# Sixteen-head attention: maxima of two heads as one pair of row tiles, and fixed groups of PSUM banks in place of a ring of three

## The chip, the core and the metric

The kernel runs on one core of a Trainium2 chip. The metric is the device time of one execution of the whole program, in microseconds (us), lower is better. The engines are TensorE (PE; its weight loads are shown apart as PEld), VectorE (DVE), ScalarE (ACT), GpSimd (POOL) and SyncE (SP). PSUM has eight banks of 512 float32 per partition; here they are `PS[:, 0]` to `PS[:, 7]`.

## The reference

Four layers of attention, cross attention and experts on `x` of 2 x 1024 x 256. The change concerns the six sublayers that run the class `Attention`: their tags are a0, a8, a9 and a11 (queries and keys are both the 1024 rows) and a4 and a10 (1024 queries, 154 keys of a context). a0 and a9 are causal; a10 has a mask. All have 16 heads of 16 elements. Cut to what they compute:

```python
q, k, v = ...                       # (b, s, 256) @ weights, split into 16 heads of 16
scores = einsum('bqhd,bkhd->bhqk', q, k) * scale    # scale is 1/4
probs = softmax(scores [+ causal or given mask])
out = einsum('bhqk,bkhd->bqhd', probs, v)
```

## The kernel before

**Precision.** A matmul of bfloat16 operands streams one column a cycle. So q and k are each cut into three bfloat16 parts (high, middle, low), and the six products of parts that matter are laid along the contraction: head h has its q in 96 rows of `qS[:, h, :]` and its k in 96 rows of `kS[:, h, :]`. Two more rows (`QH` to `QM`, 96 and 97) hold minus the row maximum in two parts in `qS`, and ones in `kS`, so that a score comes out with its maximum already taken away.

**Tiling.** A sublayer has four segments s (two batches, two halves of eight heads). A segment has four units u, (g, qb): four heads by 512 queries. A unit has steps t, one for each 128 keys: 8 without a causal mask, 4 or 8 with one, 2 where there are 154 keys. So a8 and a11 have 16 units and 128 steps, a0 and a9 have 96 steps, a4 and a10 have 32. Each step has two slots jj (two heads each).

**Pieces.** The work around the steps is cut into pieces:

- `split`: q, k, v of 128 rows for eight heads (`qkv`), read from PSUM by ACT (by DVE where there is a bias or a norm of q and k) into `A`, then cut into parts in `ST`: the high parts by ACT in segment 0 and by POOL from segment 1 on, the rest on DVE and POOL;
- `turn`: eight transposes of `ST` on PE into one bank, copied to `qS` or `kS` by ACT and DVE in turn;
- `max`: a score matmul with the queries on partitions (128 x 512 for one head), whose maximum over keys DVE takes with `tensor_reduce`;
- `fin1`, `fin2`: the maxima are cut into two parts, transposed and written to `qS`;
- `out`: the finished unit is transposed and divided by its sums.

**Order.** `place` deals the pieces to slots by position (`spread`); the maxima of unit u+1 go to slots of unit u. Every engine runs the same list. PE's slot is: two score matmuls (`pe_scores`), in the second slot of a step also the value matmuls of the step before (`pe_values`: float32, four column tiles of 32 side by side), then the slot's pieces. ACT takes the exponential of the two banks of a slot in one instruction. `self.first` comes ahead of all steps: the whole preparation of segment 0, then the maxima of unit 0, then `fin1`, `fin2`.

**Banks.** Scores use banks 0, 1 (slot 0) and 2, 3 (slot 1), values bank 4. All pieces share a ring of three, banks 5 to 7: `bank` gives `5 + use % 3`, and `wait_bank` makes PE wait until the piece three uses back has been read. A `max` piece fills one bank (or, with 154 keys, one bank with two heads side by side).

Of the kernel before, what the change touches and what calls it, by code (L numbers as in the profile page):

```python
# [15 lines left out]
S = 1024  # L16
# [428 lines left out]
class Attention(Stage):  # L445
# [12 lines left out]

    has_post = False
    lead = 0.3  # L460

    def __init__(self, K, tag, KV, causal):
# [10 lines left out]
        self.ST = [scr.take([2, 8, 104], BF16) for _ in range(3)]  # L473
# [14 lines left out]
    def place(self):  # L488
# [28 lines left out]
        order = list(self.first)  # L517
        for pieces in self.slots:
            order += pieces
        order.append(("out", len(self.units) - 1))  # L520
        self.use, self.by_use, self.turns = {}, [], {}
        for p in order:
            if p[0] != "fin1":
                self.use[p] = len(self.by_use)
                self.by_use.append(p)
            if p[0] == "turn":
                self.turns[p] = len(self.turns)
# [13 lines left out]
    def max_pieces(self, u):  # L541
        return [("max", u, i, half) for i in range(16 if self.KV == S else 8) for half in range(self.halves(u))]
# [9 lines left out]
    def bank(self, p):  # L552
        return 5 + self.use[p] % 3
# [4 lines left out]
    def wait_read(self, e, p):  # L558

        K, tag = self.K, self.tag  # L560
        on_act = (p[0] == "split" and self.bias is None and not self.has_post) or (p[0] == "turn" and self.turn_on_act(p))
        e.wait_ge(K.av if on_act else K.vv, (tag, "aux", p))
# [28 lines left out]
    def slot(self, ST, rows, z, js):  # L591
        v = ST[0:rows, z, :, 0:96].rearrange("p h (j d) -> p h j d", d=16)
# [4 lines left out]
    def dup(self, v, rows, n):  # L597
        return bc(v[0:rows].unsqueeze(2), [rows, 8, n, 16])
# [22 lines left out]
    def pe_piece(self, e, p):  # L621
# [7 lines left out]
        elif p[0] == "turn":  # L629
# [7 lines left out]
            for h in range(8):  # L637
                t = e.transpose(pb[0:104, h, 0:rows], ST[0:rows, z, h, :], K.identb[0:rows, 0:rows])
            t.then_inc(K.mm, (tag, p))
        elif p[0] == "max":  # L640
            _, u, i, half = p
            s, g, qb = self.units[u]
            b, qS, kS = s // 2, self.qS[s % 2], self.kS[s % 2]
            o = self.max_bank(p)
            self.wait_turned(e, s)
            if self.KV == S:
                qt, j = i // 4, i % 4
                h, q0 = 4 * g + j, 512 * qb + 128 * qt
                diag = self.causal and half == self.halves(u) - 1
                m = e.matmul(o, qS[0:QH, h, q0:q0 + 128], kS[0:QH, h, 512 * half:512 * half + o.shape[1]], start=True, stop=not diag)  # L650
                if diag:
                    m = e.matmul(o[:, o.shape[1] - 128:o.shape[1]], K.identb, K.maskS, start=False, stop=True)
            else:
                qt, jj = i // 2, i % 2
                q0 = 512 * qb + 128 * qt
                for k in range(2):
                    h = 4 * g + 2 * jj + k
                    m = e.matmul(o[:, KC * k:KC * k + KC], qS[0:QH, h, q0:q0 + 128], kS[0:QH, h, 0:KC], start=True, stop=self.mask is None)
                    if self.mask is not None:
                        m = e.matmul(o[:, KC * k:KC * k + KC], K.identb, self.mask[0][:, 8 * b + 4 * qb + qt, :], start=False, stop=True)  # L660
# [13 lines left out]
    def max_bank(self, p):  # L674

        _, u, i, half = p
        width = 2 * KC
        if self.KV == S:
            diag = self.causal and half == self.halves(u) - 1
            width = 128 * (i // 4 + 1) if diag else 512  # L680
        return self.K.PS[:, self.bank(p), 0:width]
# [6 lines left out]
    def pe_scores(self, e, n, jj):  # L688
        K, tag, PS = self.K, self.tag, self.K.PS
# [6 lines left out]
        if n > 0:  # L696
            e.wait_ge(K.av, (tag, "exp", n - 1, jj))
        if t == 0:
            self.wait_read(e, ("fin2", u))
        for k in range(2):  # L700
            h = 4 * g + 2 * jj + k
            o = PS[0:rows, 2 * jj + k, lo:512]
            m = e.matmul(o, self.kS[s % 2][0:QM, h, 128 * t:128 * t + rows], self.qS[s % 2][0:QM, h, q0 + lo:q0 + 512], start=True,
                         stop=not diag and self.mask is None)
            if self.mask is not None:
                m = e.matmul(o, K.identb[0:rows, 0:rows], self.mask[1][0:rows, t, b * S + q0:b * S + q0 + 512], start=False, stop=True)
            if diag:
                m = e.matmul(PS[0:rows, 2 * jj + k, lo:lo + 128], K.identb, K.maskT, start=False, stop=True)
# [32 lines left out]
    def act_piece(self, e, p):  # L741
        K, tag, PS = self.K, self.tag, self.K.PS
        if p[0] == "split":
# [26 lines left out]
            if hq:  # L770
                m = e.activation(self.slot(ST, rows, 0, [0, 1, 2]), self.dup(a[:, 0], rows, 3), ACT.Copy)
                m.then_inc(K.av, (tag, "hi" if not hk else "hi q", s, w))
# [3099 lines left out]
```

## Time and profile before

| | us |
|---|---|
| median of three runs | 7174.8 (7172.98 to 7180.21) |
| the profiled execution | 7183.6, of it 7181.8 in the span of the trace |

The profile's page gives the busy time of each engine, as a share of the span:

| engine | busy us | share |
|---|---|---|
| PE | 5763.3 | 80% |
| PEld (weight loads) | 3029.1 | 42% |
| DVE | 4253.9 | 59% |
| ACT | 2749.3 | 38% |
| POOL | 1762.4 | 25% |

PE leads, but the mean covers unlike stages. The six sublayers stand in the trace as follows (read from the order of time on PE): for each the preparation of segment 0, the maxima of unit 0, and the steps.

| tag | keys | preparation from | maxima from | steps from, to | length of the steps |
|---|---|---|---|---|---|
| a0 | 1024, causal | 39 | 70 | 80, 437 | 357 |
| a4 | 154 | 2205 | 2220 | 2227, 2397 | 171 |
| a8 | 1024 | 4512 | 4536 | 4559, 5027 | 468 |
| a9 | 1024, causal | 5490 | 5522 | 5532, 5899 | 366 |
| a10 | 154, mask | 5950 | 5975 | 5982, 6189 | 206 |
| a11 | 1024 | 6247 | 6279 | 6302, 6773 | 472 |

Together that is about 2040 us of steps and 220 us ahead of them. The other 4900 us run code that the change doesn't touch. PE's clock is shown as a granted share: 1.00 is 2.4 GHz, 0.50 is 1.2 GHz.

### The profile page before, as it was taken

To read this page: it belongs to the slowest core of one execution; us is meant where nothing else is said; L and a number is where in the kernel's file an instruction comes from. 1 tells how busy PE (TensorE), PEld (TensorE's weight loads), DVE (VectorE), ACT (ScalarE), POOL (GpSimd) and SP (SyncE) were. 2 spreads that over 40 slices of the span, in tenths; PEclk is the share of its full clock that TensorE was granted. 3 is DMA by queue.
4 is the path that set the end of the run, shared out by engine and by line. 5 is a ranking of instruction groups with operands and counts; after the bars stand their busy time and mean duration, and the time that the engine had idled before them with its cause. 6 is when DMAs were issued, how large, how long until landed. Compare 5 with 4: busy or idle time off the path is not lost. (4 is left out here: it accounts for less than half of the span.)

```text
span 7181.8 us, 69269 instructions
## 1 busy us (share of the span) xinstructions
PE 5763.3 (80%) x26178; PEld 3029.1 (42%) x26194; DVE 4253.9 (59%) x7193; ACT 2749.3 (38%) x4376; POOL 1762.4 (25%) x2107
## 2 busy tenths in 40 slices
PE   7969999999877865656566687899694887799966
PEld 4435555555534432323222255332582444433344
DVE  5664454444365469898998922777225765587622
ACT  4543333333204333333333321567112555456500
POOL 2211121211013015353444500220204213222022
PEclk9989999999888987888787886899797998899988
DMA  1000000000000000000000000000351000000022
GB/s 45 1 2 1 1 1 1 1 1 1 18 9 17 7 24 0 0 0 0 0 0 0 0 9 15 22 1 1 109 182 33 1 15 1 27 1 1 26 92 86
DMA packets 47884, 134.60 MB, mean 19 GB/s; under 512 B 4822, under 2 KB 31990, under 8 KB 41534
## 3 DMA queue, kind: packets, MB, share of 16 engines
q1 hardware_dynamic: 38094, 77.67, 3.1%
q0 software_dynamic: 9456, 52.50, 2.1%
q8 instruction: 207, 3.39, 0.2%
q14 instruction: 127, 1.04, 0.0%
HBM read 99.42 MB, written 31.20 MB: 18 GB/s over the span
## 5 line engine op out<-in xcount | busy, mean ns | idle before, releaser
L73 PE MATMUL PS<-SC 128*32 128x512 f32 (+12 forms) x11760 | 2703.7, 464 | 625.9 <-DVE SC L82 500.6
L79 ACT ACTIVATE SC<-PS 128x512 f32<-128x512 f32 (+10 forms) x2773 | 1900.8, 716 | 1967.2 <-PE PS L73 1622.1
L94 DVE TENSOR_REDUCE SC<-PS 128x1 f32<-128x512 f32 (+4 forms) x2832 | 1567.5, 594 | 697.4 <-PE PS L73 682.6
L73 PEld LDWEIGHTS PS<-SC 128*32 128x32 f32 (+5 forms) x11760 | 988.7, 122 | 1933.9 <-DVE SC L82 617.1
L73 PE MATMUL PS<-AR 128*128 128x512 f32 (+6 forms) x3902 | 1219.0, 424 | 106.9 <-DVE SC L82 55.2
L82 POOL TENSOR_TENSOR SC<-SC 128x128 bf16<-128x128 f32 (+4 forms) x764 | 935.2, 1232 | 1070.5 <-ACT SC L79 749.3
L76 PE MATMUL PS<-AR,SC 128*104 128x128 bf16 (+4 forms) x4820 | 579.4, 265 | 499.9 <-DVE SC L85 228.4
L73 PE MATMUL PS<-SC,AR 128*128 128x512 f32 (+7 forms) x1824 | 861.1, 602 | 61.9 <-DVE SC L82 20.6
L91 DVE TENSOR_TENSOR_SCAN SC<-SC 128x512 f32<-128x512 f32 (+1 forms) x544 | 885.7, 1689 | 14.9 <-ACT SC L79 3.5
L73 PEld LDWEIGHTS PS<-AR 128*128 128x128 f32 (+2 forms) x3902 | 631.7, 178 | 529.9 <-issue 334.3
L79 ACT ACTIVATE SC<-SC 128x512 f32<-128x512 f32 (+5 forms) x874 | 440.5, 561 | 1015.4 <-DVE SC L91 741.7
L76 PEld LDWEIGHTS PS<-AR,SC 128*104 128x104 bf16 (+4 forms) x4820 | 444.5, 140 | 747.7 <-issue 398.2
L73 PE MATMUL PS<-RR 97*128 97x512 f32 (+4 forms) x2048 | 630.6, 440 | 3.4 <-DVE SC L94 2.9
L73 PEld LDWEIGHTS PS<-SC,AR 128*128 128x128 f32 (+3 forms) x1840 | 387.1, 218 | 474.7 <-issue 361.2
L97 POOL CAST SC<-SC 128x256 bf16<-128x256 f32 (+2 forms) x696 | 263.1, 405 | 1212.4 <-DVE SC L82 622.0
L82 DVE TENSOR_TENSOR SC<-PS,SC 128x256 f32<-128x256 f32 (+4 forms) x529 | 239.3, 463 | 432.4 <-PE PS L73 229.1
L73 PEld LDWEIGHTS PS<-RR 97*128 97x128 f32 (+3 forms) x2048 | 372.4, 186 | 213.9 <-issue 123.0
L73 PE MATMUL PS<-AR,SC 128*128 128x256 f32 (+3 forms) x1504 | 417.6, 430 | 28.8 <-ACT SC L79 16.2
L97 POOL CAST RR<-SC 64x512 fp32r<-64x512 f32 (+1 forms) x305 | 168.5, 553 | 997.3 <-DVE SC L82 972.6
L97 DVE COPY SC<-PS 2x512 bf16<-2x512 bf16 (+7 forms) x405 | 216.4, 534 | 275.5 <-PE PS L73 139.4
L73 PEld LDWEIGHTS PS<-AR,SC 128*128 128x128 f32 (+1 forms) x1504 | 283.5, 196 | 140.0 <-issue 89.2
L82 DVE TENSOR_TENSOR SC<-SC,PS 128x2048 f32<-128x2048 f32 (+2 forms) x176 | 304.9, 1732 | 28.1 <-PE PS L73 27.0
(71 smaller groups left out, 2049.5 us busy)
## 6 DMA issues: line engine op xcount, KB each, us to landing
xg<-AR SPq DMA_DIRECT2D x20, 512.0 KB, 5.4
SC<-in_pk11e SPq DMA_DIRECT2D x8, 1152.0 KB, 6.5
SC<-in_pk11e SPq DMA_DIRECT2D x8, 1028.0 KB, 5.1
SC<-xg SPq DMA_DIRECT2D x23, 256.0 KB, 2.9
yg<-SC SPq DMA_DIRECT2D x23, 256.0 KB, 2.2
SC<-xg SPq DMA_DIRECT2D x8, 512.0 KB, 6.1
yg<-SC SPq DMA_DIRECT2D x8, 512.0 KB, 3.3
AR<-in_pk SPq DMA_DIRECT2D x2, 1562.0 KB, 8.5
```

What stands on the lines that cost most here:

```text
L73: return Step(self.real and self.real.matmul(*a, **k))
L76: return Step(self.real and self.real.transpose(*a, **k))
L79: return Step(self.real and self.real.activation(*a, **k))
L82: return Step(self.real and self.real.tensor_tensor(*a, **k))
L91: return Step(self.real and self.real.tensor_tensor_scan(*a, **k))
L94: return Step(self.real and self.real.tensor_reduce(*a, **k))
L97: return Step(self.real and self.real.tensor_copy(*a, **k))
```

## The change

**Layout.** `ST` grows from 104 to 112 columns. An even head keeps its parts in rows 0 to 95 and its maximum in 96 and 97; an odd head has its maximum in rows 0 and 1 and its parts in 16 to 111, in reversed order. With that, three of the six products (48 rows) of an even head lie in rows 0 to 47 and those of an odd head in rows 64 to 111.

**Maxima.** A `max` piece now takes two heads: one matmul on rows 0 to 47, one on rows 64 to 111. In the built program they are row tiles of 64 x 128, at positions (0, 0) and (64, 0), and write two banks. One `tensor_reduce` takes both maxima (two outputs per partition). The maximum is then that of three products of six; the same value is taken from every score of the row, so the softmax stays the same. There are 1152 such pieces in all six sublayers.

**Banks.** `queue` deals three rings: scores (banks 0, 1 and 2, 3 in turn, as before), maxima (the one pair 5, 6), and the rest, `split`, `turn`, `fin2`, `out` (the one bank 7). `wait_bank` looks two uses back for scores and one use back for the other two.

**Parts.** All instructions that cut into parts are issued for even heads and for odd heads apart: with half the elements, and twice as many.

```diff
 def bank(self, p):
-        return 5 + self.use[p] % 3
+        z, n = self.ring[p]
+        return (2 * (n % 2), 5, 7)[z]
...
 def wait_bank(self, e, p):
-        n = self.use[p] - 3
+        z, n = self.ring[p]
+        n -= (2, 1, 1)[z]
         if n >= 0:
-            self.wait_read(e, self.by_use[n])
+            self.wait_read(e, self.rings[z][n])
...
+            for k, r in ((0, slice(0, 48)), (1, slice(64, 112))):
+                h = 4 * g + 2 * jj + k
+                m = e.matmul(o[:, k, :], qS[r, h, q0:q0 + 128], kS[r, h, k0:k0 + w], start=True, stop=not diag and self.mask is None)
+            for k in range(2):
+                if self.mask is not None:
+                    m = e.matmul(o[:, k, :], K.identb, self.mask[0][:, 8 * b + 4 * qb + qt, :], start=False, stop=True)
                 if diag:
-                    m = e.matmul(o[:, o.shape[1] - 128:o.shape[1]], K.identb, K.maskS, start=False, stop=True)
+                    m = e.matmul(o[:, k, w - 128:w], K.identb, K.maskS, start=False, stop=True)
...
 def max_bank(self, p):
+        return self.K.PS[:, self.bank(p):self.bank(p) + 2, 0:width]
...
 def act_piece(self, e, p):
-            if hq:
-                m = e.activation(self.slot(ST, rows, 0, [0, 1, 2]), self.dup(a[:, 0], rows, 3), ACT.Copy)
...
-            if hk:
-                e.activation(self.slot(ST, rows, 1, [0, 3]), self.dup(a[:, 1], rows, 2), ACT.Copy).then_inc(K.av, (tag, "hi k", s, w))
-                e.activation(self.slot(ST, rows, 1, [5]), a[0:rows, 1], ACT.Copy).then_inc(K.av, (tag, "hi", s, w))
+            for odd in range(2):
+                if hq:
+                    e.activation(self.slot(ST, rows, 0, odd, [1, 2, 3]), self.some(a, rows, 0, odd, 3), ACT.Copy).then_inc(
...
+                if hk:
+                    e.activation(self.slot(ST, rows, 1, odd, [0, 2, 4]), self.some(a, rows, 1, odd, 3), ACT.Copy).then_inc(
...
 def dve_piece(self, e, p):
-                e.tensor_reduce(m2[:, i // 4, i % 4, half:half + 1], o, AX.X, ALU.max).then_inc(K.vv, (tag, "aux", p))
...
+            e.tensor_reduce(self.m2[u % 2][:, qt, 2 * jj:2 * jj + 2, half], self.max_bank(p), AX.X, ALU.max).then_inc(K.vv, (tag, "aux", p))
```

Apart from this, the scratch of the first norm and one row of biases get other places in memory.

**PE, steps of a8 between two preparations.** `128x512` with a wait for DVE is a `max` matmul, `128x512` with a wait for ACT opens the two score matmuls of a slot, `32x512 x4` are the value matmuls. Before:

```order
L73 MATMUL PS<-SC 128x512 [waits s_dve_results] x2
L73 MATMUL PS<-SC 128x512 [waits s_act_results]
L73 MATMUL PS<-SC 128x512
L73 MATMUL PS<-SC 32x512 x4
L73 MATMUL PS<-SC 128x512 [waits s_dve_results] x2
L73 MATMUL PS<-SC 128x512 [waits s_act_results]
L73 MATMUL PS<-SC 128x512
```

With the change:

```order
L73 MATMUL PS<-SC 128x512 [waits s_act_results]
L73 MATMUL PS<-SC 128x512
L73 MATMUL PS<-SC 32x512 x4
L73 MATMUL PS<-SC 128x512 [waits s_dve_results]
L73 MATMUL PS<-SC 128x512
L73 MATMUL PS<-SC 128x512 [waits s_act_results]
L73 MATMUL PS<-SC 128x512
L73 MATMUL PS<-SC 128x512 [waits s_dve_results]
L73 MATMUL PS<-SC 128x512
```

Where two maxima stood, each with a wait on the read three uses back, there is one pair of row tiles with one wait, on the read of the pair just before it.

**PE, preparation of segment 0 in a8.** `128x384` is the `split`, `104x128` (`112x128`) the eight transposes of a `turn`. Before:

```order
L73 MATMUL PS<-AR 128x384 [waits s_act_results]
L73 MATMUL PS<-AR 128x384
L76 MATMUL PS<-AR,SC 104x128 [waits s_pool_results,s_act_results]
L76 MATMUL PS<-AR,SC 104x128 x7
L76 MATMUL PS<-AR,SC 104x128 [waits s_dve_results]
L76 MATMUL PS<-AR,SC 104x128 x7
```

With the change:

```order
L73 MATMUL PS<-AR 128x384 [waits s_dve_results]
L73 MATMUL PS<-AR 128x384
L76 MATMUL PS<-AR,SC 112x128 [waits s_pool_results,s_act_results]
L76 MATMUL PS<-AR,SC 112x128 x7
L76 MATMUL PS<-AR,SC 112x128 [waits s_act_results]
L76 MATMUL PS<-AR,SC 112x128 x7
```

The order is the same, but every wait now names the reader of the piece just before: a split waits for DVE's copy of the turn ahead of it, the second turn for ACT's copy of the first.

**ACT, preparation of segment 0 in a0.** `128x8x16` and `128x256` read a split from PSUM, the next rows write its high parts, `98x8x128` (`112x8x128`) copies a turn. Before:

```order
L79 ACTIVATE SC<-PS 128x8x16
L79 ACTIVATE SC<-PS 128x256
L79 ACTIVATE SC<-SC 128x8x48
L79 ACTIVATE SC<-SC 128x8x2x16
L79 ACTIVATE SC<-SC 128x8x16
L79 ACTIVATE SC<-PS 98x8x128
```

With the change:

```order
L79 ACTIVATE SC<-PS 128x8x16
L79 ACTIVATE SC<-PS 128x256
L79 ACTIVATE SC<-SC 128x4x48
L79 ACTIVATE SC<-SC 128x4x3x16
L79 ACTIVATE SC<-SC 128x4x48
L79 ACTIVATE SC<-SC 128x4x3x16
L79 ACTIVATE SC<-PS 112x8x128
```

Between the read of a split and the copy of a turn stand four instructions in place of three, each with 192 elements per partition.

## Rows read from the trace of the kernel before

**Rows 1.** Stretches: length, busy us of each engine (count), granted clock, DMA, GB/s
```profile
4700.00:4800.00 100.00, 96.64 (x593) 34.20 (x591) 76.94 (x134) 67.78 (x81) 20.55 (x51) 1.00 0.00 1
```

**Rows 2.** Groups of DVE by shape, whole span: count, busy us, mean ns, idle before
```profile
L94 DVE TENSOR_REDUCE SC<-PS 128x1 f32<-128x512 f32 x1920 | 1246.9, 685 | 530.1 <-PE PS L73 522.9
L94 DVE TENSOR_REDUCE SC<-PS 128x2 f32<-128x308 f32 x256 | 112.6, 474 | 39.7 <-PE PS L73 36.8
L94 DVE TENSOR_REDUCE SC<-SC 128x64 f32<-128x1024 f32 x8 | 9.8, 1220 | 0.3
```

**Rows 3.** Order of time, PE, a8: start, us, instruction
```profile
4670.14 0.38 PE L73 MATMUL PS<-SC 98*128 98x512 bf16 x1
4670.45 0.64 PE L73 MATMUL PS<-SC 128*32 128x512 f32 x4
...
4671.45 0.39 PE L73 MATMUL PS<-SC 96*128 96x512 bf16 x1
```

**Rows 4.** Order of time, first maxima of a8, PE and DVE
```profile
4536.14 0.38 PE L73 MATMUL PS<-SC 96*128 96x512 bf16 x1 [0.88 <-DVE SC L97]
...
4536.55 0.69 DVE L94 TENSOR_REDUCE SC<-PS 128x1 f32<-128x512 f32 x1 [0.56 <-PE PS L73]
...
4537.30 0.10 PEld L73 LDWEIGHTS PS<-SC 96*128 96x128 bf16 x1 [0.85 <-DVE SC L94]
```

**Rows 5.** Order of time, PE where tile sizes change, a10 and a0
```profile
6183.30 0.39 PE L73 MATMUL PS<-SC 98*26 98x512 bf16 x1
6183.61 0.38 PE L73 MATMUL PS<-SC,AR 26*26 26x512 bf16 x1
...
275.61 0.70 PE L73 MATMUL PS<-AR,SC 64*128 64x256 f32 x2
276.24 0.34 PE L73 MATMUL PS<-SC 98*128 98x384 bf16 x1
```

**Rows 6.** Order of time, PE: `out` pieces of a8, then a4; unit ends of a0
```profile
4727.01 0.55 PE L76 MATMUL PS<-AR,SC 128*128 128x128 f32 x3 [0.21 <-DVE SC L94]
...
4849.10 0.55 PE L76 MATMUL PS<-AR,SC 128*128 128x128 f32 x3 [0.21 <-DVE SC L94]
...
4936.02 0.55 PE L76 MATMUL PS<-AR,SC 128*128 128x128 f32 x3 [0.21 <-DVE SC L94]
...
4961.70 0.55 PE L76 MATMUL PS<-AR,SC 128*128 128x128 f32 x3 [0.21 <-DVE SC L94]
...
2361.70 0.52 PE L76 MATMUL PS<-AR,SC 128*128 128x128 f32 x3 [0.39 <-ACT SC L79]
2369.64 0.52 PE L76 MATMUL PS<-AR,SC 128*128 128x128 f32 x3 [0.39 <-ACT SC L79]
...
270.85 0.69 PE L73 MATMUL PS<-SC 128*32 128x128 f32 x9
366.47 0.69 PE L73 MATMUL PS<-SC 128*32 128x128 f32 x9
```

**Rows 7.** Order of time, preparation of a8, PE, then ACT
```profile
4523.81 1.51 PE L73 MATMUL PS<-AR 128*128 128x384 f32 x4
4525.28 1.10 PE L76 MATMUL PS<-AR,SC 128*104 128x128 bf16 x16
4526.22 1.51 PE L73 MATMUL PS<-AR 128*128 128x384 f32 x4
...
4520.88 0.52 ACT L79 ACTIVATE SC<-SC 128x384 bf16<-128x384 f32 x1
...
4521.62 0.29 ACT L79 ACTIVATE SC<-SC 128x128 bf16<-128x128 f32 x1
4521.82 1.00 ACT L79 ACTIVATE SC<-PS 98x1024 bf16<-98x1024 bf16 x1
```

**Rows 8.** Stretches of 8 us in a4 and in the first maxima of a8
```profile
2352.00:2360.00 8.00, 6.23 (x53) 2.88 (x56) 5.99 (x18) 5.79 (x8) 0.00 (x0) 1.00 0.00 0
4544.00:4552.00 8.00, 8.00 (x14) 1.36 (x13) 8.00 (x14) 0.00 (x0) 0.00 (x0) 0.50 0.00 0
```

More of the change, by code:

```diff
@@ L516, in place, with queue, read_by_act @@
         self.first = self.prep(0) + self.max_pieces(0) + [("fin1", 0), ("fin2", 0)]
[L517 to L527, printed above, removed]
+        self.ring, self.rings, self.turns = {}, ([], [], []), {}
+        for p in self.first:
+            self.queue(p)
+        for n in range(len(self.steps)):
+            for jj in range(2):
+                self.queue(("score", n, jj))
+                for p in self.slots[2 * n + jj]:
+                    self.queue(p)
+        self.queue(("out", len(self.units) - 1))
+    def queue(self, p):
+        if p[0] == "turn":
+            self.turns[p] = len(self.turns)
+        if p[0] != "fin1":
+            z = {"score": 0, "max": 1}.get(p[0], 2)
+            self.ring[p] = (z, len(self.rings[z]))
+            self.rings[z].append(p)
+    def read_by_act(self, p):
+        return (p[0] == "split" and self.bias is None and not self.has_post) or (p[0] == "turn" and self.turn_on_act(p))
     def spread(self, pieces, a, b, rank=0):
@@ L560, in wait_read @@
         K, tag = self.K, self.tag
-        on_act = (p[0] == "split" and self.bias is None and not self.has_post) or (p[0] == "turn" and self.turn_on_act(p))
-        e.wait_ge(K.av if on_act else K.vv, (tag, "aux", p))
+        if p[0] == "score":
+            e.wait_ge(K.av, (tag, "exp", p[1], p[2]))
+            return
+        e.wait_ge(K.av if self.read_by_act(p) else K.vv, (tag, "aux", p))
         if p[0] == "fin2":
@@ L644, in pe_piece @@
             o = self.max_bank(p)
+            w = o.shape[2]
+            q0, k0 = 512 * qb + 128 * qt, 512 * half
+            diag = self.causal and half == self.halves(u) - 1
             self.wait_turned(e, s)
[L646 to L650, printed above, removed]
[L651 to L660 removed]
+            for k, r in ((0, slice(0, 48)), (1, slice(64, 112))):
[4 more added lines that the diff above has]
+                    m = e.matmul(o[:, k, :], K.identb, self.mask[0][:, 8 * b + 4 * qb + qt, :], start=False, stop=True)
+                if diag:
+                    m = e.matmul(o[:, k, w - 128:w], K.identb, K.maskS, start=False, stop=True)
             m.then_inc(K.mm, (tag, p))
@@ new lines, in pool_piece @@
+        e.wait_ge(K.gv, (tag, "mid k" if hk else "mid q", 1, s, w))
+        for odd in range(2):
+            if hq:
+                m = e.tensor_tensor(self.slot(ST, rows, 0, odd, [4]), self.some(a, rows, 0, odd, 1), self.slot(ST, rows, 0, odd, [0]), ALU.subtract)
+                m.then_inc(K.gv, (tag, "parts" if odd and not hk else ("lo q", odd), s, w))
+            if hk:
+                m = e.tensor_tensor(self.slot(ST, rows, 1, odd, [3]), self.some(a, rows, 1, odd, 1), self.slot(ST, rows, 1, odd, [1]), ALU.subtract)
+                m.then_inc(K.gv, (tag, "parts" if odd else "lo k", s, w))
```

116 lines of the change are left out of this document (57 added, 59 removed).

## The prediction, made before the changed kernel was timed

> **What bounds the kernel now.** I first cut the span into stretches of 100 us. In the steps of a8, PE is busy for 96.6 of 100 us at the full clock, and DVE for 76.9 [rows 1]; a11 reads alike. So PE sets the pace of the two sublayers without a causal mask, with DVE not far behind. Next the order of time within a step. A 512-column matmul streams 0.21 us at 2.4 GHz; the value matmuls of a step take 1.00 us from their start to the next piece's, and they start 0.31 us after a score matmul that streams 0.21 [rows 3]. Four scores, four maxima, values: 1.7 + 0.1 + 1.0, about 2.9 us, and a unit of eight steps without preparation takes 25.7 us from one `out` to the next; four units, three of them with preparation, take 122.1 [rows 6]. Then the groups of DVE by shape: a reduce of 512 takes 0.685 us, of 308 0.474, and one of 1024 columns 1.22 (from SBUF, but 0.685 plus 512 times the slope between the first two, 1.03 ns, gives 1.22 as well) [rows 2].
>
> What lets PE stay busy is the ring of three banks: PE makes two more maxima while DVE reads one. In the first maxima of a8, where nothing else runs, a reduce starts 0.41 us after its matmul does, and PE's next weight load comes 0.06 us after the reduce that freed the bank (4536.55 + 0.69 to 4537.30) [rows 4].
>
> **The change, part by part.**
>
> *Pairs.* PE drops 1152 maxima matmuls' worth of streaming if the two row tiles run side by side: 640 of 512 columns (0.213 us each), 256 causal ones of 320 on average, 256 of 154. That is 136 + 34 + 16 = 186 us of PE work. That row tiles overlap is not in the trace; the nearest are the column tiles of the values: four float32 matmuls within 0.64 us [rows 3], where one alone would stream 0.43 or more. I take them as side by side and bound it by one after the other.
>
> *Tile sizes.* A pair is 64 x 128 between 128-row matmuls. In a10, matmuls that alternate between tile sizes start 0.31 us apart in place of 0.21: 0.10 us for each change of size. In a0 two float32 matmuls on 64 rows take 0.63 us, no more than four 128-column ones beside them, so the price may be zero [rows 5]. I take 0.10. A step of a8 has two changes now (around the values) and five then: 0.3 us more against 0.43 saved. So PE's own gain is a third of what it looks like, 0 to 0.43 us a step.
>
> The Trainium skill, TensorEngine Tiling (Array Packing), Tiling Modes, says that a change of tiling mode, unlike a change of tile, drains TensorE. The rows of a10 agree (0.10 us), those of a0 leave it open. By the rule nearly nothing of PE's gain is left; without it 0.3 us a step would be, but in a chain that DVE paces that moves the sum little.
>
> *One pair of banks for maxima.* This is the term that decides. PE can't start a pair before DVE has read the last. From pair to pair: 0.44 us to the reduce's start (0.41 and a little for the second tile), 1.22 for 1024 columns, 0.09 back to PE: **1.75 us**, whatever PE does meanwhile. PE behind that wait holds up scores, values, exponentials. Sixteen pairs are 28.0 us a unit, more than the 25.7 a unit takes now. And the pairs aren't evenly loaded: where only two scores stand between them, PE needs 0.22 + 0.10 + 0.43 + 0.10 = 0.85 and waits 0.9; with the values 1.84, all PE. A unit without preparation, pair by pair from the order of the pieces: nine gaps of 1.75, four of 1.84, one with `fin2` 2.1, one with `out` 2.45, and one that spans three slots without maxima 3.8: **31.5 us for 25.7**. With preparation I add 1.3 for each split and 0.47 for each turn [rows 7] where they don't fit under 1.75, and 0.4 where DVE's copy of a turn goes ahead of a reduce: four units 139 for 122. Three such groups, +52; three and a half units without, +16; the start +3: 71 us for a8, 142 with a11. Bounds: 80 (only 28.0 a unit, the preparation hidden) to 190.
>
> *Causal, a0 and a9.* The diagonal pairs add two mask matmuls and two changes of size; with 128, 256, 384, 512 columns a pair takes 0.99, 1.31, 1.63, 1.95 us, so 16 pairs of a unit of eight tiles 25.8 us, 8 of a short unit 11.8. The chain is densest in each group of four units, where 32 pairs fall in 20 slots: in a0's last group 37 us pass for them now (377 to 414 in the trace, DVE busy for nearly all of it), then 2 x 25.8 and DVE's other work, 56, and 2.5 more ahead: +21.5. In the three groups with preparation, each 95.6 us [rows 6], PE's work already fills that stretch; +12 each (2 to 20). So +57 for a0, 115 with a9. Bounds 60 to 150.
>
> *154 keys, a4 and a10.* A pair is as wide as before, but the three-deep ring is gone: 0.29 + 0.474 + 0.09 = 0.85 us from pair to pair. A unit without preparation takes 7.9 us [rows 6]; then six gaps of 0.85, 2.5 with `fin2`, 2.8 with `out`: 10.3. Twenty splits and turns of a segment fall in two units, one after another in the one bank 7, each waiting some 0.6 us for ACT or DVE to read the last. +45 a sublayer, 90 for both. Bounds 35 to 130.
>
> *One bank for the rest, ahead of the steps.* Before the first step nothing hides bank 7. Now a tile of a8 takes 2.4 us (4523.81 to 4526.22) [rows 7]. Then: split 1.5, ACT's read 0.7, ACT's four high parts 1.3 (192 columns each, between 0.29 for 128 and 0.52 for 384) while PE turns, ACT's copy 1.0, second turn 0.7, DVE's copy 0.7, handovers 0.2: 6.1 us. Eight tiles, the first and last shorter: +23; the maxima of unit 0 at 1.75 for 1.2 per pair: +9. With the same count: a0 +24, a4 +16, a8 +32, a9 +33, a10 +16, a11 +34: **155**. Bounds 90 to 190.
>
> *Parts on POOL.* Twice the instructions, each for half the elements, about 1 us more per split. POOL is busy for 20.6 of 100 us in the steps [rows 1] and a split comes every 10 us or so: nothing. If that cover went, `turn` would wait for POOL.
>
> *Clock.* In the first maxima of a8, where DVE paces PE, the clock was at 0.50 (1.2 GHz); in a4, whose waits are short, at 1.00 [rows 8]. The longer start of six sublayers looks like the former: half of 155 + 36 us at the low level, where PE's part doubles, +40 (0 to 70). Whether the steps follow is a rival.
>
> **Sum.** 142 + 115 + 90 + 155 + 40 = 542 us. The profiled execution took 7183.6, so 7725; the median of the runs is 8.8 lower: **7717 us**, +7.6%.
>
> **Rivals.**
>
> - *Waits partly hidden.* Every term at its low bound: 80 + 60 + 35 + 90 + 0 = 265, so 7440. For it: sums of gaps assume that PE catches up nothing. Against: 16 times 1.75 is above a unit's time today. Chance 0.17.
> - *The clock falls in the steps too.* At 1.2 GHz a gap with values is 3.5 us and the other 1.95: 14 us more a unit. If half of the 30 units of a8 and a11 run so, and as much of a0 and a9, +310: 8030. For it: PE will stand still for half of every other gap, as in the maxima at 0.50. Against: a4's stretch at 1.00 has waits as well. Chance 0.15.
> - *The two tiles run one after the other.* Each pair 0.21 us longer in the chain, on 0.8 of them: +150, 7870. Chance 0.10.
> - *Faster.* PE's work decides alone, all 186 us are saved, and no wait for DVE shows. It needs the reduce (1.22) plus handovers to fit into PE's other work in each gap, and changes of size to be free: 6989. Decided by whether PE's work between pairs is over 1.75 us; it is so only in gaps with values. Chance 0.03.
>
> The Trainium skill, TensorE: Matmul & The Clock Gate, Packing small matmuls, reports 3.07 times for four row tiles of 512 columns, not 4. By that a pair would stream some 0.28 us (an estimate), and 1152 pairs would add at most 80 us to the chain.
>
> **Numbers.** The forecast holds 0.55. The range leaves out what lies under 7470 and over 8040, about one case in ten on either side. Under 0.2% (14 us, about what a measurement of this kernel can tell) is neither: faster 0.03, same 0.01, slower 0.96.
>
> **What the changed profile would show.** In a8: PE busy near 70% and not 97; reduces `128x2<-128x1024` near 1.22 us, 1.7 apart, each starting 0.44 us after its pair; PE idle "<- DVE L94" about 0.9 us once a step; 31 us from `out` to `out`. In the preparation: splits 6 us apart. Two row tiles starting together, or 0.21 us apart, settle that rival; the granted clock of 100 us stretches settles the other. The forecast is wrong if PE's waits for L94 sum up to little, or if a reduce of two banks takes well under 1.2 us.

## The result, and the profile after

The changed kernel takes 7994.2 us (median of four runs, 7988.05 to 8001.16) where the kernel before took 7173.9 in the same comparison: 1.114 times as long, with a 95% interval of 1.112 to 1.116. That is 820 us more; the prediction had 542 more. The profiled execution's span is 7986.1 us, against 7181.8 before.

First the whole: busy time of each engine, with the share of the span, from the page of the changed kernel.

```profile
PE 6022.7 (75%) x26178; PEld 3048.7 (38%) x26194; DVE 4236.8 (53%) x6349; ACT 2770.4 (35%) x4424; POOL 1903.6 (24%) x3097
```

The pairs were to save PE work, and PE is busy for 259 us more. So something made its work slower, beside the waits. The stretches say where: 100 us of a8, of a4 and of a0 (length, busy us with count of PE, PEld, DVE, ACT, POOL, then the granted clock).

```profile
5100.00:5200.00 100.00, 80.00 (x453) 22.83 (x454) 61.94 (x68) 54.80 (x62) 16.04 (x55) 0.91 0.00 1
2400.00:2500.00 100.00, 72.86 (x405) 35.92 (x400) 35.46 (x92) 35.93 (x43) 34.19 (x121) 0.67 0.00 1
300.00:400.00 100.00, 85.96 (x640) 39.10 (x638) 49.83 (x73) 52.56 (x78) 27.67 (x95) 0.82 0.00 1
```

In a8 PE was busy for 96.6 us of 100 and DVE for 76.9 [rows 1]; now it is 80.0 and 61.9. No engine is full any more: they wait for each other. In a4 and a0 the clock has gone too.

Cut by sublayer, the two traces give this (us; "ahead" is preparation and maxima of unit 0, the two parts of the steps are what PE is idle and what it is busy):

| tag | ahead, more by | steps before | steps after | more by | of it PE idle | of it PE busy | clock in the steps, before and after |
|---|---|---|---|---|---|---|---|
| a0 | 32.2 | 356.9 | 462.1 | 105.2 | 48.8 | 56.4 | 0.98, 0.77 |
| a4 | 19.5 | 170.7 | 286.4 | 115.7 | 47.4 | 68.3 | 0.93, 0.67 |
| a8 | 42.6 | 468.3 | 567.0 | 98.7 | 99.2 | -0.5 | 0.99, 0.93 |
| a9 | 36.8 | 367.0 | 451.8 | 84.8 | 53.1 | 31.6 | 0.98, 0.84 |
| a10 | 20.9 | 206.4 | 320.9 | 114.5 | 50.4 | 64.2 | 0.99, 0.80 |
| a11 | 40.5 | 471.9 | 565.6 | 93.7 | 99.7 | -5.9 | 0.99, 0.93 |

Sums: 193 ahead, 613 in the steps, of which 399 idle and 214 busy. The rest of the program is unchanged to a few us. (Ahead of the steps the kernel before takes 239 us by the table of its sublayers, and not the 220 that the sentence under it has.)

Now the chain, in the steps of a8. PE's order of time (start, us, instruction), then DVE's reduces in the same stretch:

```profile
5321.06 0.39 PE L73 MATMUL PS<-SC 48*128 48x512 bf16 x2 [0.78 <-DVE SC L94]
5321.38 0.39 PE L73 MATMUL PS<-SC 98*128 98x512 bf16 x1
5321.61 0.38 PE L73 MATMUL PS<-SC 112*128 112x512 bf16 x1
5321.92 0.64 PE L73 MATMUL PS<-SC 128*32 128x512 f32 x4
...
5322.92 0.39 PE L73 MATMUL PS<-SC 48*128 48x512 bf16 x2
5323.24 0.39 PE L73 MATMUL PS<-SC 98*128 98x512 bf16 x1
5323.46 0.38 PE L73 MATMUL PS<-SC 112*128 112x512 bf16 x1
5324.63 0.39 PE L73 MATMUL PS<-SC 48*128 48x512 bf16 x2 [0.78 <-DVE SC L94]
...
5321.49 1.22 DVE L94 TENSOR_REDUCE SC<-PS 128x2 f32<-128x1024 f32 x1 [0.49 <-PE PS L73]
5323.35 1.22 DVE L94 TENSOR_REDUCE SC<-PS 128x2 f32<-128x1024 f32 x1 [0.64 <-PE PS L73]
```

A pair is one row with x2 and 0.39 us, the same 0.39 that one matmul has alone: both row tiles run side by side. The score behind it starts 0.32 us later, 0.22 of streaming and 0.10 for the change of tile size. The reduce starts 0.43 us after its pair and takes 1.22, and the next pair comes 0.06 us behind it: 1.71 us from pair to pair (5322.92 to 5324.63), and 1.86 with the values between (5321.06 to 5322.92). PE's waits in the steps of a8 (in total, times, longest), now and before:

```profile
PE PS L73 <- DVE SC L94: 102.9, 123, 1.4
```
```profile
PE PS L73 <- DVE SC L94: 4.6, 23, 0.2
```

The prediction's signs, one by one: the distance of 1.75 us is there, the wait for L94 is 0.80 us a step (0.9 expected), and an `out` of a unit without preparation comes 31.2 us after the last (5362.14 and 5393.30; 31.5 expected, 25.7 before [rows 6]). PE's busy share in a8 is 80%, where near 70 was expected, and ahead of its steps a tile takes 5.7 to 7.7 us from split to split, for 6. The two `out`:

```profile
5362.14 0.33 PE L76 MATMUL PS<-AR,SC 128*128 128x128 f32 x1
...
5393.30 0.33 PE L76 MATMUL PS<-AR,SC 128*128 128x128 f32 x1
```

The granted clock is what isn't as expected. This is one unit of a4 without preparation, after and then before: the stretch, and PE's waits in it.

```profile
2630.63:2644.26 13.63, 10.03 (x49) 3.08 (x48) 5.85 (x15) 5.85 (x7) 0.00 (x0) 0.63 0.00 1
PE PS L73 <- DVE SC L94: 3.6, 5, 1.3
```
```profile
2378.66:2386.51 7.85, 6.08 (x49) 2.74 (x49) 5.41 (x15) 5.98 (x8) 0.00 (x0) 1.00 0.00 0
PE PS L73 <- ACT SC L79: 1.1, 1, 1.1
PE PS L73 <- DVE SC L94: 0.3, 1, 0.3
```

PE has 49 matmuls in both. They take 6.08 us at a clock of 1.00 (2.4 GHz), and 10.03 at 0.63, which is mostly 1.2 GHz. Of the 5.8 us that the unit grows, 4.0 are PE's own work at the lower clock (by estimate 6.08 us at 0.63 would be 9.7), and the waits are only the rest.

### The profile page after: what moved, and what is told of

It reads as the page before. It is cut to its first block and busy times, and to the rows that moved or that the text cites. A ratio compares the mean times of both kernels' runs of the same rounds, so it can differ in the third digit from the quotient of the medians.

```text
span 7986.1 us, 69289 instructions
## 1 busy us (share of the span) xinstructions
PE 6022.7 (75%) x26178; PEld 3048.7 (38%) x26194; DVE 4236.8 (53%) x6349; ACT 2770.4 (35%) x4424; POOL 1903.6 (24%) x3097
## 5 line engine op out<-in xcount | busy, mean ns | idle before, releaser
L73 PE MATMUL PS<-SC 128*32 128x512 f32 (+13 forms) x11760 | 2728.4, 503 | 1009.5 <-DVE SC L82 498.0
L94 DVE TENSOR_REDUCE SC<-PS 128x2 f32<-128x1024 f32 (+6 forms) x1936 | 1533.2, 802 | 1227.5 <-PE PS L73 1221.7
L73 PEld LDWEIGHTS PS<-SC 128*32 128x32 f32 (+6 forms) x11760 | 905.3, 124 | 2435.8 <-DVE SC L94 786.7
L73 PE MATMUL PS<-AR 128*128 128x512 f32 (+6 forms) x3902 | 1260.2, 448 | 176.6 <-DVE SC L82 81.2
L82 POOL TENSOR_TENSOR SC<-SC 128x64 bf16<-128x64 f32 (+4 forms) x1256 | 1005.2, 822 | 1078.2 <-ACT SC L79 744.9
L76 PE MATMUL PS<-AR,SC 128*112 128x128 bf16 (+4 forms) x4820 | 659.0, 288 | 589.2 <-DVE SC L85 229.8
L76 PEld LDWEIGHTS PS<-AR,SC 128*112 128x112 bf16 (+4 forms) x4820 | 497.7, 160 | 889.6 <-issue 428.9
L79 ACT ACTIVATE SC<-SC 128x512 f32<-128x512 f32 (+6 forms) x918 | 444.4, 543 | 1043.3 <-DVE SC L91 741.9
L97 POOL CAST SC<-SC 128x128 bf16<-128x128 f32 (+2 forms) x1176 | 326.7, 318 | 1697.1 <-DVE SC L82 897.7
L82 DVE TENSOR_TENSOR SC<-PS,SC 128x256 f32<-128x256 f32 (+5 forms) x465 | 219.9, 478 | 446.2 <-PE PS L73 240.5
```

The source lines that it names most:

```text
L73: return Step(self.real and self.real.matmul(*a, **k))
L76: return Step(self.real and self.real.transpose(*a, **k))
L79: return Step(self.real and self.real.activation(*a, **k))
L82: return Step(self.real and self.real.tensor_tensor(*a, **k))
L94: return Step(self.real and self.real.tensor_reduce(*a, **k))
L97: return Step(self.real and self.real.tensor_copy(*a, **k))
```

## The experiments

The change has four parts: who shares which bank, two heads read by one reduce, row tiles in place of full rows, and the finer cutting into parts. The runs take them one at a time. Six of them and the changed kernel stand in this table (us; the kernel before was 7172 to 7178 beside them; the run with full rows and two heads has the layout and the parts of the kernel before):

| maxima matmul | piece | ring of three (banks 5 to 7) | maxima 5, 6 and the rest 7 |
|---|---|---|---|
| full rows | one head | 7264 | 7675 |
| full rows | two heads, one reduce | | 8058 |
| row tile | one head | 7515 | 7950 |
| row tiles | two heads | 7555 (two reduces) | 7994 (one reduce, the changed kernel) |

**Banks alone.** The kernel before, its layout and full rows, with the changed kernel's pieces of two heads and its groups of banks.

```diff
-        return 5 + self.use[p] % 3
+        z, n = self.ring[p]
+        return (2 * (n % 2), 5, 7)[z]
...
+            for k in range(2):
+                h = 4 * g + 2 * jj + k
+                m = e.matmul(o[:, k, :], qS[0:QH, h, q0:q0 + 128], kS[0:QH, h, k0:k0 + w], ...)
```

> The kernel before, with its layout, its six products on 96 rows, and its way of cutting into parts, but with the changed kernel's pieces of two heads, one reduce of two banks, and its groups of banks (maxima 5 and 6, the rest 7). The banks part of the change alone. Theory (banks are the cost): the two matmuls of a pair run one after the other, so pair to pair is 0.65 + 1.22 + 0.09 = 1.96 us in a8; steps of a8 550 to 600 (468 before, 567 changed); 7900 to 8150 us. Rival (row tiles or the parts are the cost): 7174 to 7500.

Measured: 8058.2 us, 1.122 (1.120 to 1.124). The banks part alone costs 886 us, more than the whole change. Steps of a8, then of a9 (stretch, then PE's waits):

```profile
4873.03:5473.97 600.94, 476.83 (x2616) 152.32 (x2617) 339.08 (x369) 320.31 (x375) 78.39 (x192) 0.93 0.00 1
PE PS L73 <- DVE SC L94: 108.6, 120, 1.3
...
6016.11:6483.90 467.79, 370.62 (x2568) 163.98 (x2569) 250.66 (x385) 208.16 (x287) 78.92 (x192) 0.84 0.00 1
PE PS L73 <- DVE SC L94: 64.9, 81, 1.8
```

a8 takes 601 us, just over the expected 550 to 600. There is no row tile here, and the clock of a9 is at 0.84 as in the changed kernel: waits by themselves are enough to lower it.

**The ring of three back, row tiles kept, one head a piece.**

```diff
-            z = {"score": 0, "max": 1}.get(p[0], 2)
+            z = {"score": 0}.get(p[0], 1)
...
-        return (2 * (n % 2), 5, 7)[z]
+        return (2 * (n % 2), 5 + n % 3)[z]
...
-        n -= (2, 1, 1)[z]
+        n -= (2, 3)[z]
...
+            r, h = (slice(0, 48), slice(64, 112))[j % 2], 4 * g + j
+            m = e.matmul(o, qS[r, h, q0:q0 + 128], kS[r, h, k0:k0 + w], ...)
```

> The changed kernel, but a maxima piece is one head (one row tile, one bank, one reduce of 512 or less), even and odd head next to each other, and all pieces share one ring of three banks again, as before the change. Only row tiles, three products and the finer cutting into parts stay. Theory (the fixed groups of banks cost the time: a pair waits 1.22 us of reduce with nothing else to write, and bank 7 alone holds up the preparation): PE's waits for DVE's reduces fall from 103 us to under 15 in the steps of a8, preparation takes what it took before, clock back near 0.98; 7150 to 7250 us. Rival (row tiles and their changes of tile size are the cost): waits fall, but PE's busy time goes up, 7400 or more. Second rival (row tiles save 186 us of PE work as soon as waits are gone): 7050 or less.

Measured: 7514.8 us, 1.048 (1.046 to 1.050). The waits went as the theory said (5.0 us for L94 in a8), and 480 us came back, but not the other 340. The first rival is nearer: row tiles have a price of their own. The next run isolates it.

**The same with full rows.** Only the rows of the maxima matmul differ from the run above.

```diff
-            r, h = (slice(0, 48), slice(64, 112))[j % 2], 4 * g + j
+            r, h = slice(0, 112), 4 * g + j
```

> As the run with one head a piece over the ring of three (7515 us), but the maxima matmuls take all 112 rows of a head in place of a row tile of 48: the rows of the maximum still hold zeros then. Same pieces, same banks, same waits, same layout and same cutting into parts; no row tiles and no change of tile size around the maxima. Theory (row tiles themselves cost in that run: they run one after another, each group of them between two changes of tile size, and the clock of a0, a4, a9 and a10 falls with them): steps of a8 back to 468 to 472, clock of a0 and a9 back to 0.98, 7180 to 7240 us. Rival (the cutting in two halves and the odd heads' layout cost it): 7400 or more.

Measured: 7263.8 us, 1.012 (1.010 to 1.013). 251 us are the row tiles'. Steps of a9, with row tiles and then with full rows:

```profile
5665.90:6110.42 444.52, 422.00 (x2568) 164.39 (x2569) 264.69 (x569) 208.22 (x287) 99.49 (x336) 0.81 0.00 1
PE PS L73 <- DVE SC L94: 9.0, 26, 0.9
```
```profile
5588.97:5957.04 368.07, 323.26 (x2568) 147.02 (x2569) 259.53 (x569) 205.74 (x287) 99.72 (x336) 0.99 0.00 1
PE PS L73 <- DVE SC L94: 15.9, 49, 0.9
```

Both have 2568 matmuls on PE. With row tiles PE waits less for the reduces (9.0 us for 15.9), and still the clock is 0.81 in place of 0.99 and the steps are 76 us longer. So more waits aren't needed for a low clock: row tiles between full-row matmuls bring it too. In a8 the clock stays at 0.99 with both, and the steps are 481.1 and 469.1. With full rows a0, a8, a9 and a11 take what they took before (359.0, 469.1, 368.1, 471.3), so the new layout and the finer parts cost next to nothing in the steps, as predicted; outside all steps the two traces differ by 13 us. The 86 us that this run is slower than before are mostly in a4 and a10, 41 and 27 us, where one head a piece makes two reduces of 154 columns (0.314 us each) out of one of 308 (0.477) and takes two places of the ring for one. That this is the reason wasn't tested.

**The groups of banks, one head a piece.** With row tiles, and with full rows:

```diff
-        return (2 * (n % 2), 5, 7)[z]
+        return (2 * (n % 2), 5 + n % 2, 7)[z]
...
-        n -= (2, 1, 1)[z]
+        n -= (2, 2, 1)[z]
```

> The changed kernel with its own groups of banks (scores 0 to 3, maxima 5 and 6, the rest 7), but a maxima piece is one head with one bank and a reduce of its own, so a bank comes free 0.69 us after its reduce starts and not 1.22. Theory (the chain of pair, reduce of two banks, pair is what holds PE up in the steps): two reduces take 1.37 us a pair and each bank has its own chain of 0.41 + 0.69 + 0.09 = 1.19, so the chain is shorter than PE's own work in a8: waits for reduces fall from 103 to under 30 us, steps of a8 from 567 to about 490, a11 the same; a0 and a9 some 50 less each, and the clock follows; preparation in segment 0 unchanged (bank 7 is): 7600 to 7750 us. Rival (the number of banks for maxima counts, two in place of three, not how they are released): steps of a8 above 540, 7900 us.

> As the run with full-row maxima, one head a piece (7264 us), but with the changed kernel's groups of banks: scores 0 to 3, maxima 5 and 6, the rest 7. Against the run of the same groups with row tiles (7950 us) only the row tiles differ, and against the banks alone with a reduce of two banks (8058 us) only that each bank is read and freed by itself. Theory (the fixed groups cost mostly by the wait for a reduce of two banks and by bank 7, and the row tiles by PE's time and clock): a8 490 to 500, a0 and a9 375 to 390, preparation as changed, 7550 to 7650 us. Rival (two banks for maxima in place of three cost as much however they are read): 7850 or more.

Measured: 7949.9 us, 1.108 (1.106 to 1.110), and 7675.3, 1.070 (1.068 to 1.071). Both are above what I expected. Full rows first: against 8058 for the banks alone, 383 us came back with each bank read and freed by itself (the layout and the parts differ too, which cost next to nothing in the steps of the run above); a8 takes 512.6 us (490 to 500 expected). Against 7264 with the ring of three, two banks for maxima and one for the rest still cost 411. With row tiles the theory failed: 44 us came back, not 250 to 400, and a8 takes 542.9 us, as the rival had it (above 540), though by another way than the rival's. PE's waits for L94 in a8 did fall, to 47 us, but its busy time rose from 451 to 486. Each tile now waits for its own bank, and only 89 times in a8 do two row tiles start together, against 240 in the changed kernel. Where they don't, it looks like this:

```profile
5345.06 0.39 PE L73 MATMUL PS<-SC 48*128 48x512 bf16 x1 [0.24 <-DVE SC L94]
5345.65 0.39 PE L73 MATMUL PS<-SC 48*128 48x512 bf16 x1 [0.21 <-DVE SC L94]
```

**Bank 7 ahead of the steps.** The changed kernel, with the preparation of segment 0 dealt over banks 5, 6, 7.

```diff
         z, n = self.ring[p]
+        if z == 2 and n < self.ahead:
+            return 5 + n % 3
...
-        n -= (2, 1, 1)[z]
+        n -= 3 if z == 2 and n < self.ahead else (2, 1, 1)[z]
```

> The changed kernel, but the preparation of segment 0, ahead of all steps, deals its splits and turns over the three banks 5, 6, 7, which nothing else uses then. Theory (ahead of the steps the one bank 7 is what costs): a tile of a8 falls from 7.7 us to about 2.5 to 3.5, the six preparations lose 100 to 146 us together, nothing else moves: 7850 to 7900 us. Rival (twice as many instructions for the parts on ACT, DVE and POOL are the cost, or the clock): a tile stays at 6 us or more, 7950 to 7994.

Measured: 7849.7 us, 1.094 (1.092 to 1.096), 144 less than the changed kernel: as expected, and so is the tile of a8. In the changed kernel one tile stretches from split to split, 7.66 us; here it is 2.62 (PE, start, us):

```profile
4796.55 2.93 PE L73 MATMUL PS<-AR 128*128 128x384 f32 x4 [0.78 <-DVE SC L97]
...
4800.12 1.10 PE L76 MATMUL PS<-AR,SC 128*112 128x128 bf16 x8 [0.64 <-ACT SC L79]
...
4802.33 1.10 PE L76 MATMUL PS<-AR,SC 128*112 128x128 bf16 x8 [1.11 <-ACT SC L79]
...
4804.21 1.01 PE L73 MATMUL PS<-AR 128*128 128x384 f32 x1 [0.79 <-DVE SC L97]
```
```profile
4747.89 1.51 PE L73 MATMUL PS<-AR 128*128 128x384 f32 x4
...
4749.57 1.10 PE L76 MATMUL PS<-AR,SC 128*112 128x128 bf16 x16 [0.17 <-ACT SC L79]
...
4750.51 1.51 PE L73 MATMUL PS<-AR 128*128 128x384 f32 x4
```

Three waits a tile (0.64, 1.11, 0.78) are gone, and the split takes 1.51 us and not 2.93: with the waits the clock came back as well.

**Pairs side by side over three banks.** Row tiles in pairs again, but a pair takes two places of the ring and has two reduces.

```diff
+            self.rings[z].extend([p + (0,), p + (1,)] if p[0] == "max" else [p])
...
-        return (2 * (n % 2), 5, 7)[z]
+        return (2 * (n % 2), 5 + (n + k) % 3)[z]
...
+        for m in (n, n + 1)[0:2 if p[0] == "max" else 1]:
```

> The changed kernel, with its pairs of row tiles, but all pieces share the ring of three banks again, a pair takes two places of it, and DVE reads each head with a reduce of its own, so that the next pair can start when the first of two banks is read. Against the run with one head a piece (7515 us, a8's steps 481) only this differs: the two matmuls of a pair stand next to each other without a wait between them. Theory (row tiles run side by side only when nothing stands between them, and then save 0.43 us a step against three more changes of tile size of 0.10): a8 and a11 take about 450 in place of 481, a0 and a9 some 10 to 15 less, 7420 us, and the rest of the distance to 7174 is the clock in the causal sublayers and those with 154 keys. Rival (the two tiles do not overlap at all): 7500 to 7530.

Measured: 7555.4 us, 1.054 (1.052 to 1.056): slower than one head a piece. Steps of a8, pairs and then single heads:

```profile
4712.67:5218.88 506.21, 436.93 (x2617) 131.74 (x2617) 351.96 (x609) 319.75 (x375) 99.01 (x336) 0.96 0.00 1
PE PS L73 <- DVE SC L94: 58.9, 112, 0.9
```
```profile
4674.96:5156.05 481.09, 466.03 (x2616) 136.55 (x2617) 347.04 (x609) 320.33 (x375) 98.70 (x336) 0.99 0.00 1
PE PS L73 <- DVE SC L94: 5.0, 24, 0.4
```

PE's work did shrink, by 29 us, as the tiles run side by side. It is given back in waits: a pair needs two of three banks at once. I had compared PE's work with its own work only, and forgotten that the third bank is what hid the reduce.

**Hybrid, and another order on PE.** The kernel before in a0, a4, a9 and a10; in a8 and a11 pairs over the ring of three. The second of these runs then also changes PE's order within a step:

```diff
             for jj in range(2):
                 self.pe_scores(e, n, jj)
-                if jj == 1 and n > 0:
-                    self.pe_values(e, n - 1)
-                for p in self.slots[2 * n + jj]:
-                    self.pe_piece(e, p)
+            for p in self.slots[2 * n]:
+                self.pe_piece(e, p)
+            if n > 0:
+                self.pe_values(e, n - 1)
+            for p in self.slots[2 * n + 1]:
+                self.pe_piece(e, p)
```

> The kernel before in a0, a4, a9 and a10, and in a8 and a11 the changed layout with pairs of row tiles, but over the ring of three banks with a reduce for each head. Theory: as the run with pairs over three banks in a8 and a11 (about 450 in place of 468 and 472) and as before elsewhere: 7130 to 7160 us, faster than both. Rival (the parts in two halves and the changes of tile size take the gain): 7175 to 7210.

> As the run that has the kernel before in a0, a4, a9, a10 and pairs over three banks in a8 and a11 (7267 us), but in a8 and a11 PE's step is both slots' scores, a pair, the values, a pair, in place of scores, pair, scores, values, pair. The distance from pair to pair is then 1.3 to 1.4 us both times and no longer 0.85 and 1.84. Theory (that run lost to uneven gaps: a pair needs two of three banks, and where only two scores stand between pairs PE waits 0.5 us for DVE): waits for reduces fall from 60 us to under 25, a step goes to 2.8 to 2.95 us, steps of a8 and a11 to 430 to 450: 7110 to 7140 us, faster than before. Rival (DVE, 1.37 us a pair and more with its other work, becomes the bound, or the clock falls): a8 470 or more, 7180 to 7270.

Measured: 7266.6 us, 1.013 (1.011 to 1.015), slower than theory and rival alike, and 7182.8, 1.0006 (0.9997 to 1.0015). The uneven gaps were most of the cause in the first: with even ones the waits halve (59.7 to 27.7 us in a8), and the steps go from 505.2 to 464.3, where the kernel before has 468.3. The theory's 430 to 450 isn't reached, though:

```profile
4933.00:4981.95 48.95, 44.39 (x272) 11.81 (x272) 45.24 (x79) 34.57 (x39) 0.00 (x0) 1.00 0.00 1
```

These are two units without preparation, 24.5 us each (25.7 before). DVE is busy for 45.2 us of 49 and PE for 44.4: as the rival had it, DVE's two reduces a pair are the next bound, close behind PE.

**First maxima over the score banks.** As the last run, and the 16 pairs ahead of the steps of a8 and a11 use banks 0 to 3, with one reduce each.

```diff
+            z = 2 if p[0] == "max" and p[1] == 0 else {"score": 0}.get(p[0], 1)
...
-        return (2 * (n % 2), 5 + (n + k) % 3)[z]
+        return (2 * (n % 2), 5 + (n + k) % 3, 2 * (n % 2) + k)[z]
```

> As the run with the other order in a8 and a11 (7183 us), but the maxima of unit 0 in these two, ahead of the steps, take the score banks 0, 1 and 2, 3 in turn, which are free until the first step, with one reduce of two banks for a pair. Theory (these 16 pairs are bound by DVE: 1.22 us in place of two times 0.69, and no wait for a third bank): the maxima take 20 to 21 us in place of 26.4, and 22.6 in the kernel before: 7170 us, 0.1% under the kernel before, together with the 4 and 6 us that the other order saved in the steps. Rival (the chain of PE and DVE is what counts there, and the clock at 1.2 GHz): 24 us or more, 7180.

Measured: 7175.3 us beside 7175.2 for the kernel before, ratio 0.9998 (0.9989 to 1.0007). The first maxima of a8 fell from 26.4 to 21.5 us, those of a11 from 27.0 to 21.6. Of these 10 us some 5 show in the total (the run above was 4.7 us over the kernel before beside it, this one is level with it); the gain over the kernel before can't be told from none. This is the best version found, and it does not beat the kernel before.

**Does more work keep the clock up?** The changed kernel, with every score matmul of a4 and a10 issued twice.

```diff
+            for again in range(2 if self.KV != S else 1):
+                m = e.matmul(bank[:, lo:512], ...)
```

> The changed kernel, but in a4 and a10 every score matmul is issued twice with the same operands (the second overwrites the first), four more matmuls a step of 512 columns: 27 us more PE work in each of the two at the full clock, 55 at half. Everything else is as changed. Theory (in a4 and a10 most of the loss is the clock, which falls because PE stands still between short pieces of work): more work keeps the clock up, PE busy no more than now, steps of a4 from 286 to 240-265 and of a10 from 321 to 280-300, 7900 to 7950 us: more work, less time. Rival (the waits alone cost the time, and the clock falls for another reason): a4 and a10 get 27 to 55 us longer each, 8050 to 8100.

Measured: 8041.6 us, 1.122 (1.120 to 1.123), 47 more than the changed kernel. Steps of a4, twice and then once:

```profile
2381.41:2686.02 304.61, 228.83 (x1233) 97.89 (x1233) 105.93 (x276) 108.59 (x126) 68.55 (x240) 0.73 0.00 1
PE PS L73 <- DVE SC L94: 39.5, 56, 1.4
```
```profile
2383.61:2670.05 286.44, 208.71 (x1104) 91.78 (x1105) 106.05 (x276) 108.05 (x126) 68.68 (x240) 0.67 0.00 1
PE PS L73 <- DVE SC L94: 39.4, 56, 1.4
```

My theory falls. The clock rose a little, 0.67 to 0.73 and in a10 0.80 to 0.83, and the added work, 27 us in each at the full clock, cost 18 and 30 us: some 9 were won back in a4 and none in a10, far from a gain. The waits for L94 are the same to 0.1 us: filling in matmuls ahead of a wait does not remove the wait.

## Why the prediction was right in kind and short in size

The measured 7994 us lie in the stated range of 7470 to 8040, near its upper end and 277 over the forecast of 7717. The parts, one by one:

**One pair of banks (142 forecast, 192 measured).** The chain was right in each part: 0.43 + 1.22 + 0.06 for 0.44 + 1.22 + 0.09, a unit without preparation at 31.2 for 31.5. So were the last four units, three and a half with maxima: they grew by 16.0 us as the sum has it (though 3.5 times 5.8 is 20). The group of four units that hold preparation was mis-sized. From one `out` to the fourth after it the two full ones take 148.2 and 145.9 us (5034.34, 5182.58, 5328.52) for 139, where 122.1 and 121.1 passed before, and the first one with the start grew by 31.6 for 20. That is the 28 us missing in a8 and, alike, the 23 in a11. In the two full groups PE's busy time is within 2 us of what it was; it is idle for 56.7 us, 50.4 of them in waits for L94 and 6.4 in waits of the transposes. The banks alone, without any row tile, cost more than the whole change, which shows the term to be the one that decides.

**Causal, a0 and a9 (115 forecast, 190 measured).** The last group is +23 for +21.5. The groups with preparation take 119.5 and 118.9 us in a0 from `out` to `out` for 93.3 and 94.3, so +26 and +25 and not +12; in a9 they are +19. The step that failed is the sentence that PE's work already fills that stretch. It did so at the full clock. Two units of a0 that hold preparation, after and before:

```profile
363.73:400.38 36.65, 27.92 (x170) 13.00 (x170) 17.04 (x23) 11.23 (x21) 18.94 (x65) 0.68 0.00 1
400.38:435.22 34.84, 29.10 (x170) 14.87 (x168) 16.15 (x23) 12.13 (x20) 9.89 (x35) 0.60 0.00 1
```
```profile
274.04:300.97 26.93, 24.31 (x171) 13.20 (x172) 17.82 (x38) 11.17 (x21) 14.03 (x35) 0.87 0.00 1
300.97:323.32 22.35, 20.21 (x168) 11.04 (x169) 16.74 (x35) 11.25 (x19) 8.70 (x21) 1.00 0.01 1
```

PE's busy time in the two goes from 44.5 to 57.0 us: 12.5 of the group's 25.

**154 keys (90 forecast, 230 measured).** The largest miss. From pair to pair it is 0.88 us (2638.59 to 2639.47) for 0.85, but a unit is 13.6 and not 10.3. The step that failed is in the part on the clock: I read the 1.00 of a4 [rows 8] as a sign that short waits don't lower it. The waits there were short and few; the changed kernel's are not (39.4 us for L94 in 286, and 10.4 more for bank 7), and the clock is 0.67. In the whole steps of a4 and a10 the idle time grew by 98 us, close to the 90 forecast, and 132 are PE's slower work.

**Ahead of the steps (155 and 40 for the clock forecast, 193 measured).** Right in sum, and that by luck: two errors cancel. Where the clock was high a tile took 5.7 us (4783.82 to 4789.52), for 6.1. The chain is the one forecast, ACT's four high parts in it, only they took 1.0 us for 1.3 and its read of the split 0.6 for 0.7: ACT's copy of the turn starts right behind the fourth part, and PE's last transpose was done 0.35 us before that (ACT, then PE):

```profile
4786.00 1.12 ACT L79 ACTIVATE SC<-SC 128x192 bf16<-128x192 f32 x4
4787.02 1.00 ACT L79 ACTIVATE SC<-PS 112x1024 bf16<-112x1024 bf16 x1
...
4786.02 0.65 PE L76 MATMUL PS<-AR,SC 128*112 128x128 bf16 x8 [0.64 <-POOL SC L97]
```

Most tiles of a8 ran at 1.2 GHz and took 7.7 us. So the chain was over-sized by 0.4 us a tile and the clock under-sized. The run over three banks gave 144 back.

**Pairs and tile sizes.** Row tiles ran side by side, 0.10 us a change was right (5321.06 to 5321.38, of which 0.22 are the columns), and so was that little of the gain is left. On the change of mode the Trainium skill, TensorEngine Tiling (Array Packing), Tiling Modes, says that it drains TensorE; the 0.10 us of these rows fits that. The 3.07 times that the Trainium skill has for four row tiles (TensorE: Matmul & The Clock Gate, Packing small matmuls) isn't tested here: no run has more than two row tiles side by side. What I missed is that row tiles lower the clock in the four sublayers with short matmuls. That the parts cost nothing in the steps was right.

**Clock and rivals.** The rival that came true beside the forecast is "the clock falls in the steps too". Its 8030 us is nearer to the 7994 measured than the forecast is, but partly by luck: its price of 310 us was put on a8, a11, a0 and a9, and what PE's busy time grew by in all steps is 214 us, 132 of it in a4 and a10, where I had none. In a8 and a11 busy time is unchanged only in sum: with pairs at a clock of 0.98 PE's work was 418 us (the run with the other order), and the changed kernel's 451 at 0.93 hold the saving and the clock's price, about 33 us each.

Two things lower the clock in a0, a4, a9 and a10. Waits do it without row tiles, and row tiles do it without more waits, in separate runs. For the changed kernel, where both are, the banks alone come nearest: their clock is 0.81, 0.73, 0.84 and 0.82 in the four, against 0.98, 0.93, 0.98 and 0.99 before and 0.77, 0.67, 0.84 and 0.80 in the changed kernel. So most of the fall is there without a row tile. The shares don't add up, though: with one head a piece in the same groups of banks, full rows keep a0 and a9 at 0.98 and 0.96, and row tiles bring them to 0.76 and 0.79. What stays open is the price of each in us: no run held the clock fixed.

## What to carry to other kernels

Before a ring of buffers is split into groups, write down for each group how long one use keeps it (producer's start to reader's start, the read, the hand-over) and compare that with the producer's work between two uses at the place where that work is smallest; one read over two banks holds both for the whole read. Price what an engine then does at the lower clock too, even in sublayers whose clock was nearly full: here the growth of PE's busy time in the steps was a quarter of the loss. A tile that uses part of the array is paid back only if its partner runs beside it, if both their banks are free, and if the pairs are evenly spaced.

## What the runs showed of the hardware that I had not expected

Row tiles of 48 rows among full-row matmuls lowered the granted clock with no added wait: 0.81 for 0.99 in a9, 0.91 for 1.00 in a0, 0.74 for 0.84 in a4 and 0.87 for 0.98 in a10, but 0.99 for 0.99 in a8, where the matmuls are 512 columns wide. PE's busy share in a9 was 95% with the low clock and 88% with the high one, so a high busy share in a profile is no sign of a high clock. The full rows are 112 rows of the array and the tile is 48: whether it is the change of tile size or the fewer rows at work that lowers the clock, no run tells.

Two row tiles that stand next to each other in PE's order don't always run side by side. In the run with one head a piece over the ring of three, both cases stand within a microsecond (PE, then a reduce of DVE):

```profile
5091.98 0.39 PE L73 MATMUL PS<-SC 48*128 48x512 bf16 x2
...
5092.85 0.39 PE L73 MATMUL PS<-SC 48*128 48x512 bf16 x1
5093.16 0.39 PE L73 MATMUL PS<-SC 48*128 48x512 bf16 x1
...
5092.41 0.69 DVE L94 TENSOR_REDUCE SC<-PS 128x1 f32<-128x512 f32 x1 [0.52 <-PE PS L73]
```

The first two start together; the second two 0.31 us apart, with no wait in PE's rows. It is a wait all the same. The bank of the last tile is that of the first, three uses back, and DVE's read of that one ends at 5093.10; the tile starts 0.06 us later, the same hand-over as from a reduce to the next pair. The tile ahead of it counts as busy until 5093.23, and so no idle time shows. In a8 of this run 49 of 71 second tiles that start within 0.35 us of the first start 0.04 to 0.07 us behind the end of a reduce, and in the groups of banks with one head a piece 26 of 26. A wait that is shorter than the matmul ahead of it must be looked for in the times of its reader.
